# A fused attention and FFN block on one core: queries transposed by DMA instead of by TensorE, the norm on ScalarE, the iteration in another order

## What is computed

```python
def _L0_cond_ref(hidden_states, language_ids, W1, b1, W2, b2, gamma, beta):
    h = jax.nn.relu(jnp.einsum('bsh,bha->bsa', hidden_states, W1[language_ids]) + ...)
    x = hidden_states + jnp.einsum('bsa,bah->bsh', h, W2[language_ids]) + ...
    normed = (x - mean) * jax.lax.rsqrt(var + LN_EPS)
    return normed * gamma[language_ids][:, None, :] + beta[language_ids][:, None, :]

def _L0_attn_ref(x, segment_pos, Wq, Wk, Wv, Wf, bf):
    q = (x @ Wq.T).reshape(b, t, NUM_HEADS, HEAD_DIM)
    k = x @ Wk.T
    v = x @ Wv.T
    logits = jnp.einsum('btnh,bsh->bnts', q, k) * scale
    probs = softmax(causally masked logits)
    out = jnp.einsum('bnts,bsh->btnh', probs, v).reshape(b, t, WIDTH)
    return out @ Wf.T + bf

x = x + _L0_attn_ref(_L0_cond_ref(x, ...), ...)
x = x + _L0_ffn_ref(_L0_cond2_ref(x, ...), ...)
```

## Time and profile before

| what | value |
|---|---|
| median of 3 runs | 1156.55 us (1156.05 to 1162.35) |
| profiled execution, its own time | 1157.74 us |
| its span, first to last instruction | 1156.0 us |
| TensorE busy | 1117.5 us (97%) |
| VectorE busy | 804.4 us (70%) |
| ScalarE busy | 594.7 us (51%) |
| GpSimd busy | 214.6 us (19%) |

### The profile page before, as it was taken

One profiled execution on the slowest core, in us unless ns is written; L12 is line 12 of the kernel. 1 busy time (PEld: TensorE's weight loads), 2 busy tenths in 40 slices (PEclk: granted clock), 3 DMA queues, 4 the chain that ended last, 5 costly groups with the idle time before them and its releaser, 6 DMA issues.

```text
span 1156.0 us, 18793 instructions
## 1 busy us (share of the span) xinstructions
PE 1117.5 (97%) x6148; PEld 892.6 (77%) x6178; DVE 804.4 (70%) x1440; ACT 594.7 (51%) x989; POOL 214.6 (19%) x266
## 2 busy tenths in 40 slices
PE   4899999999998999999999999999999999999998
PEld 3567777777775788888888888888888888888886
DVE  2877777776776557756577875778656887568875
ACT  1355655555555634533365654556445565455653
POOL 2233333343345444452000000000000000000000
PEclk9999999999999999999999999999999999999999
DMA  4342122122143456654515443044440444304420
GB/s 122 111 149 60 53 59 63 48 60 63 47 160 124 151 187 202 227 188 150 204 35 164 140 167 115 10 164 146 162 137 0 163 146 163 137 8 145 145 91 37
DMA packets 66765, 135.97 MB, mean 118 GB/s; under 512 B 13793, under 2 KB 28017, under 8 KB 66545
## 3 DMA queue, kind: packets, MB, share of 16 engines
q1 hardware_dynamic: 57696, 114.49, 30.5%
q10 hardware_dynamic: 9024, 20.97, 5.0%
HBM read 107.65 MB, written 30.41 MB: 119 GB/s over the span
## 4 chain that ended last, share of the span: by engine, by line
PE 89%; DVE 6%; SPq 2%; issue 1%; DMA 1%; ACT 1%; POOL 0%; DVEq 0%; POOLq 0%; ACTq 0%
PE bank L1531 35%; PE bank L1493 10%; PE bank L1319 7%; PE bank L1543 5%; PE bank L1469 4%; PE bank L1463 4%; PE bank L1253 4%; PE bank L1234 3%; DVE neg_max L891 2%; PE bank L1274 2%; PE bank L1311 2%; PE bank L1216 2%; PE bank L1200 2%; PE bank L1237 1%; PE bank L1189 1%
## 5 line engine op out<-in xcount | busy, mean ns | idle before, releaser
L1531 PE MATMUL bank<-op_lo,w_ring 128*128 128x512 f32 x896 | 348.6, 389 | 0.0
L1531 PE MATMUL bank<-op_hi,w_ring 128*128 128x512 f32 x896 | 348.6, 389 | 0.0
L1066 DVE TENSOR_TENSOR op_lo<-x_blk,op_hi 128x512 fp32r<-128x512 f32 x288 | 193.8, 684 | 30.4 <-ACT op_hi L764 30.3
L764 ACT ACTIVATE op_hi<-x_blk 128x512 fp32r<-128x512 f32 x288 | 162.8, 620 | 73.6 <-PE bank L1531 69.3
L1531 PEld LDWEIGHTS bank<-op_lo,w_ring 128*128 128x128 f32 x896 | 168.2, 188 | 34.9
L1531 PEld LDWEIGHTS bank<-op_hi,w_ring 128*128 128x128 f32 x896 | 168.2, 188 | 34.9
L891 DVE TENSOR_REDUCE neg_max<-bank 128x2 f32<-128x512 f32 (+1 forms) x192 | 126.0, 685 | 48.0 <-remote 39.7
L617 ACT ACTIVATE p<-bank 128x512 f32<-128x512 f32 x192 | 111.3, 599 | 71.9 <-PE bank L1253 68.2
L788 ACT ACTIVATE x_blk<-x_blk,scales 128x512 f32<-128x512 f32 x96 | 69.3, 722 | 67.0 <-DVE x_blk L1119 28.9
L1493 PE MATMUL bank<-tile_hi,ffn_w 128*128 128x512 f32 x256 | 101.5, 396 | 0.0
L1493 PE MATMUL bank<-tile_lo,ffn_w 128*128 128x512 f32 x256 | 101.5, 396 | 0.0
...
## 6 DMA issues: line engine op xcount, KB each, us to landing
...
xt<-in_x_t SPq DMA_DIRECT2D x16, 256.0 KB
xtok<-in_x_tok SPq DMA_DIRECT2D x16, 256.0 KB
resid<-in_x_t SPq DMA_DIRECT2D x16, 256.0 KB, 3.1
x_scratch<-x SPq DMA_DIRECT2D x16, 256.0 KB, 2.6
...
```

Source lines behind the costliest of these rows:

```text
L764: nc.scalar.activation(op_hi[:, o % OP_RING, k], x_blk[:, operand_home(o), k], ACT.Copy).then_inc(s["op_hi"], 1)
L1066: nc.vector.tensor_tensor(op_lo[:, o % OP_RING, k], x_blk[:, operand_home(o), k], op_hi[:, o % OP_RING, k].bitcast(F32), ALU.subtract).the ...
L1531: last = mm(banks[first_bank + m][:, :], w, read(v[:, q % OP_RING, k, :]), start=k == 0 and v is op_hi and i not in (P2, P3), stop=k == KB ...
```

## The change

- Queries are now projected with the head dimension on partitions (project_queries writes 2 x 128 rows by 256 tokens into ring bank 0; the columns of wq are reordered for it). ScalarE writes the high part (queries_high), VectorE the low part (queries_low), and six DMAs on SyncE's queue (move_queries: high, low, high, each for two halves of heads, 128 KB each) put them into q_t. The 16 transposes and 4 ScalarE copies are gone.
- Keys and values come from one product (wkv); ScalarE copies it to SBUF (keys_copied) and writes the keys for both halves (keys_high), VectorE the low rows (keys_low); two transposes bring the values to tokens on partitions (values_transposed), VectorE copies them out (values_of). GpSimd's copies of keys, values and queries are gone.
- The norm is applied by ScalarE with a scale and a bias; GpSimd makes the bias (shift = -mean x rstd) with two more small operations.
- q_t, keys and values have three buffers each; the loop has 4 rounds of 3 iterations instead of 6 of 2.
- The order within an iteration is rewritten on all engines, SyncE's too: load_front is split, its second half is issued first, move_maxima comes ahead of load_resid and store_x1, and the comb and ffn_scratch transfers come behind all of the pipeline's filling. In the last iteration the store of chunk 0 is issued by ScalarE after the maxima have landed.

```diff
-            iteration(-1, 1, True, True, False, False)
+            iteration(-1, 2, True, True, False, False)
             iteration(0, 0, True, True, True, False)
-            with eng.Fori(0, (B - 4) // 2) as pair:
-                for step in (1, 2):
-                    iteration(2 * pair + step, step % 2, True, True, True, True)
+            with eng.Fori(0, (B - 4) // SLOTS) as third:
+                for step in (1, 2, 3):
+                    iteration(SLOTS * third + step, step % SLOTS, True, True, True, True)
             iteration(B - 3, 1, True, True, True, True)
-            iteration(B - 2, 0, False, True, True, True)
-            iteration(B - 1, 1, False, False, True, True)
+            iteration(B - 2, 2, False, True, True, True)
+            iteration(B - 1, 0, False, False, True, True)
...
+            def move_queries(n, slot):
+                sp.wait_ge(s["q_low"], n + 1)
+                settle(sp, "sp_settled")
+                for i, part in enumerate((q_high, q_rest, q_high)):
+                    for par in range(2):
+                        row = SLOT * par + HD * i
+                        sp.dma_start(q_t[slot][row:row + HD, :, :].bitcast(F32), part[:, par, :].bitcast(F32)).then_inc(s["q_moved"], 16)
...
             load_front(1)
+            sp.wait_ge(s["const_made"], 1)
+            move_queries(0, 0)
             load_front(2)
+            sp.wait_ge(s["const_made"], 3)
+            move_queries(1, 1)
+            move_maxima(0, 0)
+            load_front(3)
+            move_queries(2, 2)
+            move_maxima(1, 1)
             for c in range(2):
                 sp.dma_start(comb[c][:, A11:A11 + 3, :], hid_d[c, :, 0:3, :]).then_inc(comb_loaded[c % 2], 16)
                 sp.dma_start(comb[c][:, A21, :], hid_d[c, :, 3, :]).then_inc(comb_loaded[c % 2], 16)
-            move_maxima(0, 0)
-            load_front(3)
-            move_maxima(1, 1)
             store_ffn()
...
-            with sp.Fori(0, (B - 4) // 2) as pair:
-                for step in (1, 2):
-                    b = 2 * pair + step
-                    load_front(b + 3)
+            with sp.Fori(0, (B - 4) // SLOTS) as third:
+                for step in (1, 2, 3):
+                    b = SLOTS * third + step
+                    l = language(b + 3)
+                    load_rest(b + 3, l)
+                    load_inputs(b + 3, l)
+                    move_queries(b + 2, (step + 2) % SLOTS)
+                    move_maxima(b + 1, (step + 1) % SLOTS)
+                    load_resid(b)
                     store_x1(b - 1)
-                    load_resid(b)
-                    move_maxima(b + 1, 1 - step % 2)
             sp.wait_ge(s["x1_stored"], HEAD + 16 * BT)
             sp.dma_start(xa[:, :, :], x1_scratch[:, :, 0:TW]).then_inc(s["xa_loaded"], 16)
             load_ffn()
+            move_queries(B - 1, (B - 1) % SLOTS)
+            move_maxima(B - 2, (B - 2) % SLOTS)
+            load_resid(B - 3)
             store_x1(B - 4)
-            load_resid(B - 3)
...
             def rstd_of(n):
                 pool.wait_ge(s["veps_ready"], n + 1)
-                if isinstance(n, int) and n == 0:
-                    pool.wait_ge(s["const_made"], 5)
-                nc.gpsimd.tensor_tensor(rstd[:, :], veps[:, :], half[:, :], ALU.pow).then_inc(s["rstd_ready"], 1)
-            def high_again(n, t):
...
-            def move_keys(n, odd, late):
...
-            def move_values(n, odd, late):
...
+                if is_first(n):
+                    pool.wait_ge(s["const_made"], 2)
+                nc.gpsimd.tensor_tensor(rstd[:, :], veps[:, :], half[:, :], ALU.pow).then_inc(s["rstd_made"], 1)
+                nc.gpsimd.tensor_scalar(shift[:, :], moments[:, :, 0], -1.0, None, ALU.mult).then_inc(s["rstd_made"], 1)
+                pool.wait_ge(s["rstd_made"], 2 * (n + 1))
+                nc.gpsimd.tensor_tensor(shift[:, :], shift[:, :], rstd[:, :], ALU.mult).then_inc(s["rstd_ready"], 1)
...
+            def normalise(n):
+                act.wait_ge(s["rstd_ready"], n + 1)
+                for t in range(NT):
+                    nc.scalar.activation(norm[:, t, :], u[:, t, :], ACT.Identity, bias=shift[:, t:t + 1], scale=rstd[:, t:t + 1]).then_inc(s["norm_ready"], 1)
...
-            def queries_out(n, odd, t, j):
...
+            def queries_high(n):
+                act.wait_ge(s["q_mm"], n + 1)
+                if not is_first(n):
+                    act.wait_ge(s["q_moved"], 96 * n)
+                nc.scalar.activation(q_high[:, :, :], ring[0][:, :].rearrange("p (a t) -> p a t", a=2), ACT.Copy, scale=QSCALE).then_inc(s["q_hi"], 1)
+            def keys_copied(n):
+                act.wait_ge(s["kv_mm"], n + 1)
+                if not is_first(n):
+                    act.wait_ge(s["keys_out"], 2 * n)
+                nc.scalar.activation(kv[:, :], ring[1][:, 0:T], ACT.Copy).then_inc(s["kv_out"], 1)
+            def keys_high(n, slot):
+                act.wait_ge(s["kv_out"], n + 1)
+                for par in range(2):
+                    nc.scalar.activation(keys[slot][:, par, :], kv[:, :], ACT.Identity,
+                                         bias=key_row[:, 2 * par:2 * par + 1], scale=key_row[:, 2 * par + 1:2 * par + 2]).then_inc(s["keys_hi"], 1)
...
-                if softmax:
-                    for u in range(0, 4):
-                        exponential(b, u)
-                if maxima:
-                    queries_out(b + 1, 1 - odd, 1, 0)
-                    queries_out(b + 1, 1 - odd, 1, 1)
-                if softmax:
-                    for u in range(4, 8):
-                        exponential(b, u)
+                if softmax and not maxima:
+                    act.wait_ge(s["maxima_moved"], 64 * B)
+                    store_chunk(0)
+                if softmax:
+                    exponential(b, 0)
+                    exponential(b, 1)
+                if front:
+                    normalise(b + 2)
+                if softmax:
+                    exponential(b, 2)
+                    exponential(b, 3)
                 if front:
                     affine(b + 2)
+                if softmax:
+                    exponential(b, 4)
+                if front:
+                    queries_high(b + 2)
+                if softmax:
+                    exponential(b, 5)
+                    exponential(b, 6)
...
+            def keys_low(n, slot):
+                dve.wait_ge(s["keys_hi"], 2 * (n + 1))
+                for par, rows in enumerate((slice(32, 64), slice(96, 128))):
+                    nc.vector.tensor_tensor(keys[slot][rows, par, :], kv[rows, :], keys[slot][rows, par, :].bitcast(F32),
+                                            ALU.subtract).then_inc(s["keys_out"], 1)
+            def queries_low(n):
+                dve.wait_ge(s["q_hi"], n + 1)
+                nc.vector.scalar_tensor_tensor(out=q_rest[:, :, :], in0=ring[0][:, :].rearrange("p (a t) -> p a t", a=2), scalar=QSCALE,
+                                               in1=q_high[:, :, :].bitcast(F32), op0=ALU.mult, op1=ALU.subtract).then_inc(s["q_low"], 1)
+            def values_of(n, slot):
+                dve.wait_ge(s["v_t_mm"], n + 1)
+                if n in (0, 1, 2) if isinstance(n, int) else False:
+                    dve.wait_ge(s["const_made"], 3 + 2 * SLOTS)
+                src, at = ring[1][:, T:2 * T].rearrange("p (t c) -> p t c", t=NT), 0
+                for row, rows in V_ROWS:
+                    nc.vector.tensor_copy(values[slot][:, :, at:at + rows], src[:, :, row:row + rows]).then_inc(s["values_out"], 1)
+                    at += rows
...
+            def project_queries(n, tail):
                 pe.wait_ge(s["norm_t_out"], n + 1)
+                if tail:
+                    pe.wait_ge(s["late_out"], n - 2)
+                elif not is_first(n):
+                    pe.wait_ge(s["q_low"], n)
+                for m in range(KD):
+                    for k in range(KD):
+                        last = mm(ring[0][:, m * T:(m + 1) * T], wq[:, k, m * P:(m + 1) * P], norm_t[:, k, :], start=k == 0, stop=k == KD - 1)
+                last.then_inc(s["q_mm"], 1)
+            def project_keys(n, tail):
+                if tail:
+                    pe.wait_ge(s["early_out"], n - 2)
+                elif not is_first(n):
+                    pe.wait_ge(s["values_out"], 2 * n)
                 for k in range(KD):
-                    last = mm(side[0][:, 0:T], wk[:, k, :], norm_t[:, k, :], start=k == 0, stop=k == KD - 1)
-                last.then_inc(s["keys_mm"], 1)
-            def project_queries(n, t, tail):
...
-            def queries_transposed(n, t, j, tail):
...
+                    last = mm(ring[1][:, 0:T], wkv[:, k, :], norm_t[:, k, :], start=k == 0, stop=k == KD - 1)
+                last.then_inc(s["kv_mm"], 1)
+            def values_transposed(n):
+                pe.wait_ge(s["kv_out"], n + 1)
+                for t in range(NT):
```

(5 more changed lines are left out.)

392 lines of the change are left out of this document (165 added, 227 removed).

## The result

The changed kernel takes 1162.58 us in the median of eight runs (1160.69 to 1167.16); the kernel before took 1156.43 beside it, in eight as well. The ratio is 1.0048, with a 95% interval of 1.0033 to 1.0062: slightly slower, at the edge of what can be told from no change, where 1135 was forecast. The profiled execution took 1164.43 us around a span of 1162.6.

What follows compares the result with a forecast made beforehand. TensorE, busy for 97% of the span, was taken as the bound. From 1157.7 us: -27.0 (13 iterations), +3.0, -1.7, +7.5 and -3.0 give 1136.5, so 1135 for the median; 8-in-10 range 1122 to 1149.

Steps and rivals of the forecast that it cites:

- L = 2.5: Query moves: the last 128 KB move lands 2.5 us after its issue, or 3.1 by the port rule; hidden in full iterations.
- Rival 3: Query moves land late, so the first maximum unit waits every iteration; at L = 6 about 1175 us; chance 0.08.
- 15.9 + L: Attention loop: least period in us, from first maximum unit through the moves' landing L; begins to bind at L = 3.7.
- The work taken from TensorE: Full attention iterations: TensorE work falls 1.59 us, from 20.5 to 18.9; period 19.6 instead of 21.68.
- the walk: New order of one iteration followed: TensorE waits 0.5 us before norm_transposed and 0.1 at project_queries.
- Rival 2: Attention loop: in-order waits from variance to project_queries are longer, period 20.6 us, +13, total 1148; chance 0.2.
- rival 4: Attention loop: removed transposes only turn into waits, 21.3 us or more per iteration, total 1155 to 1160; chance 0.07.
- The ends of the pipeline: Pipeline's start, moves exposed: sample 0 +4.2 us, iteration -1 near 18, iteration 0 some 17.8 for 19.0; together +3.0.
- (a): SyncE's queue, iteration 1: comb and ffn_scratch delay loads and moves; TensorE waits 5.5 us, plus 2 for half rate: +7.5.
- Rival 1: No collision: comb and ffn_scratch drain side by side with the loads at no cost, total 1127.5 us; chance 0.17.
- (b): Last maxima on SyncE's queue: stores and residual come later, removing the 2.78 us wait and a little clock: -3.0 us.
- iteration 14's -1.7: Last part of the attention phase: iteration 14 loses its 16 transposes, -1.7 us.

Runs made afterwards that it cites:

- e1: Changed kernel without the two moves of the second copy of the high halves, four moves instead of six (incomplete scores): 1135.69 us, 0.9813 of the kernel before.
- e14: Changed kernel, each move writing 16 rows, every eighth instead of neighbouring (not the reference's layout): 1135.91 us, 0.9817 of the kernel before.
- e16: Changed kernel, full computation, queries at every eighth row, with key weights' columns and per-row factors following: 1134.54 us, 0.9801 of the kernel before.
- e18: Changed kernel, full computation, queries at every second row within the old quarters of 32 rows: 1135.2 us, 0.9814 of the kernel before.
- e5: Changed kernel with the three moves of the odd heads issued on ScalarE's queue: 1158.48 us, 0.9999 of the kernel before.
- e6: Changed kernel, each move into 32 neighbouring rows and half of the pairs (not the reference's layout): 1144.74 us, 0.9891 of the kernel before.
- e2: Changed kernel, the same six moves each into all 128 rows of q_t (not the layout the products expect): 1128.11 us, 0.9755 of the kernel before.
- e4: Changed kernel with comb loads behind sample 0's queries and the ffn_scratch store behind sample 0's maxima: 1157.35 us, 0.9997 of the kernel before.
- e8: Kernel before with only move_maxima put ahead of load_resid and store_x1, in the loop and last iterations: 1153.38 us, 0.9956 of the kernel before.

## Why the prediction was wrong

**The step that failed is "I take L = 2.5"**, the landing of a 128 KB move after the last issue. It measured 5.05 us, outside the bounds of 1.94 and 3.1, which were rows of moves and loads with other targets: one row for each of the maxima's small moves, and all 128 rows for the loads. Rival 3 had the mechanism and the formula. With L = 5.05 its "15.9 + L" gives 21.0, and 20.9 to 21.03 was measured; its break-even, no faster from L = 4.9, held. It got a chance of 0.08, since I weighed it by rows that do not have the target's shape.

**Why L is 5.05.** Most of it above a spread move's 2.4 us is a backlog, and a part is the move's own time. Taken one by one, the six moves of the iteration above took 3.3, 3.7, 4.1, 4.5, 4.9 and 5.0 us from issue to landing; the first and the last:

```profile
q_t<-q_high SPq DMA_DIRECT2D x1, 128.0 KB, 3.3
...
q_t<-q_high SPq DMA_DIRECT2D x1, 128.0 KB, 5.0
```

Even the first took longer than the upper bound of 3.1. From the first issue to the first unit at the start of the pipeline, six moves take 8.5 us and four (e1) take 6.3, so each costs 1.1 us, some 120 GB/s. Six cost 6.6, and in an iteration they are issued within 3.3 us, each 0.65 after the last: each lands some 0.4 us later after its issue than the one before it, the last one 1.7 us later than the first. With spread rows (e14, e16, e18) each lands 2.4 to 2.5 us after its own issue, the last like the first, and no backlog builds up: a move then costs no more than the 0.65 us of an issue. A second queue (e5) doesn't shorten it.

The Trainium skill, DMA: Bandwidth & Descriptors, "The descriptor swizzle" and "Bandwidth", has the rule: groups of four rows share 16 ports, an estimated 1.2 us for 128 KB into the four ports of 16 neighbouring rows. The runs agree in size, 1.1 us. The prediction weighed this rule, and added one move's time to L where six stand in line. By the same rule 32 neighbouring rows (e6) reach eight ports, as many as the spread rows of e14, e16 and e18. Those landed in 2.4 to 2.5 us, and e6 took 3.6. So how many groups of four rows a move touches isn't what counts either: e6 and e18 touch 8, e14 and e16 touch 16. (The expectation of e18 counted 8 for every eighth row.) What makes neighbouring rows slow stays open beyond that, and no run shows the ports themselves.

**The work taken from TensorE.** With the moves out of the way the period is 19.2 to 19.3 us (e1, e2, e14, e16), forecast 19.6 between 18.9 and 20.6. The windows of one full iteration, before and in e16, show what it is made of:

```profile
151.33:173.00 21.67, 21.28 (x167) 15.82 (x167) 15.75 (x37) 12.21 (x24) 8.14 (x13) 1.00 0.18 55
...
155.83:175.02 19.19, 19.19 (x154) 14.04 (x153) 14.08 (x31) 12.54 (x25) 5.83 (x10) 1.00 0.37 104
```

TensorE's busy time falls by 2.1 us, where the sum had -1.59, and no wait is left in this iteration of e16, where the walk had 0.6. The count of work was short (20.5 for 21.28 before, 18.9 for 19.19 after) and the waits were too long; that the period came out so near is in part luck. Rival 2 is refuted by the same runs, rival 4 too. TensorE's wait for ScalarE's norm ahead of norm_transposed was foreseen, as 0.5 us; the changed kernel's trace has 0.28, and e16's none.

**The ends of the pipeline**, +3.0, came to +15.5. Sample 0's first unit is 6.8 us late where I had 4.2; iteration -1 takes 23.4 us where I wrote "stays near 18"; iteration 0 takes 22.3 for 17.8. The long landing is in each of them, and behind it the clock of 0.50 and 0.74; half rate behind a wait I had priced only in term (a). With e16's landing the same point is +7.0: sample 0 is then as forecast (+4.0), but TensorE still waits 3.75 us for it, the granted clock is 0.50 in 32 to 42 us there too, and iterations -1 and 0 take 20.5 and 19.5 us. So even with the short landing this term was too small, by 4 us.

**(a) the collision**, +7.5, was the right place and mechanism, with other sizes: iterations 1 and 2 take 24.1 and 24.2 us, some 3 us more each than the others. The wait in iteration 2 is 3.25 us, forecast 5.5, and behind it the granted clock is 0.72 in 104 to 116 us. Without the collision 5.9 us of the time go (e4). Rival 1 is refuted. **(b) the last maxima**, -3.0, with iteration 14's -1.7: the end gained 6.2 us for 4.7, the wait is gone, and e8 shows the effect on its own.

**The sum.** With spread rows the changed kernel takes 1134.5 us (e16), where 1135 was forecast. Part of that is luck: its loop gained 22.5 us for 19.5, its end 7.6 for 4.7, and its start lost 7.0 for 3.0.
